# The opening and the last pair of a conditional-residual kernel: a bias row spread by TensorE, a new order of first transfers and products, and one copy moved ahead of a store

## What is computed

```python
x = x + einsum('bct,bcd->bdt', x, weights[subjects]) + bias[subjects][:, :, None]
x = x + einsum('btd,od->bto', x, W) \
      + einsum('btr,bor->bto', einsum('btd,brd->btr', x, A[adapter]), Bm[adapter]) * scalings[adapter]
```

## Time and profile before

| what | before |
|---|---|
| median of three executions | 241.67 us |
| the profiled execution's own time | 241.36 us |
| its span, first to last instruction | 239.6 us |
| TensorE (PE) matmul, busy | 229.4 us, 96% |
| VectorE (DVE) / ScalarE (ACT) / GpSimd (POOL), busy | 149.2 / 107.9 / 79.6 us |
| granted TensorE clock, mean | 0.996 |
| DMA, bytes and mean rate | 36.64 MB, 153 GB/s |

### The profile page before, as it was taken

How to read it: one execution, slowest core, us unless ns; L and a number is a source line. 1 busy time by engine, 2 the same in 40 slices (tenths; PEclk the granted TensorE clock), 3 DMA queues, 4 the chain that set the end, 5 groups by cost and what they waited for, 6 DMA issues and landing times.

```text
span 239.6 us, 9653 instructions
## 1 busy us (share of the span) xinstructions
PE 229.4 (96%) x2900; PEld 187.7 (78%) x2901; DVE 149.2 (62%) x259; ACT 107.9 (45%) x185; POOL 79.6 (33%) x277
## 2 busy tenths in 40 slices
PE   1899999999999999999999999999999999999992
PEld 1787878888887888888888888888788888888761
DVE  6799848873358636875258835875448754425762
ACT  3184663543436363562436354454435434344441
POOL 4467771700077610610056730525135131000000
PEclk9999999999999999999999999999999999999998
DMA  5956455736565474645555574645646364562233
GB/s 132 279 169 193 141 176 156 198 94 176 148 197 141 120 213 131 201 108 192 134 154 163 147 215 109 192 115 160 172 135 191 109 200 110 155 178 63 83 78 90
DMA packets 23723, 36.64 MB, mean 153 GB/s; under 512 B 6162, under 2 KB 6162, under 8 KB 23698
## 3 DMA queue, kind: packets, MB, share of 16 engines
q1 hardware_dynamic: 16480, 26.10, 40.0%
q10 hardware_dynamic: 7218, 10.23, 13.7%
HBM read 19.53 MB, written 16.78 MB: 152 GB/s over the span
## 4 chain that ended last, share of the span: by engine, by line
PE 89%; DVE 2%; DMA 2%; ACTq 2%; issue 1%; ACT 1%; DVEq 0%
PE ps L883 69%; PE ps L843 14%; PE ps L819 3%; DMA o_ring<-in_L_cond_W_dram 2%; PE ps L764 1%; ACTq L693 1%; PE ps L775 1%; DVE o_ring L554 1%; ACT x_hi L658 1%; ACT m_f L681 1%; DVE x_lo L534 0%; PE ps L813 0%; DVE last_parts L539 0%; PE ps L871 0%; DVE o_ring L549 0%
## 5 line engine op out<-in xcount | busy, mean ns | idle before, releaser
L883 PE MATMUL ps<-m_hi,x_hi 128*128 x244 | 97.0, 398 | 0.0
L883 PE MATMUL ps<-m_hi,x_lo 128*128 x244 | 95.1, 390 | 0.0
L883 PE MATMUL ps<-m_lo,x_hi 128*128 x244 | 95.1, 390 | 0.0
L534 DVE TENSOR_TENSOR x_lo<-x,x_hi 128x512 fp32r<-128x512 f32 x64 | 44.7, 698 | 62.8 <-ACT x_hi L658 62.4
L374 POOL COPY p_pair<-p_all 64x64 f32 x128 | 42.8, 335 | 113.8 <-DVE x L526 96.9
L658 ACT ACTIVATE x_hi<-x 128x512 fp32r<-128x512 f32 x64 | 40.4, 632 | 56.0 <-ACT o_ring L671 30.9
L671 ACT ACTIVATE o_ring<-ps 128x512 f32<-128x512 f32 x60 | 35.9, 598 | 52.1 <-PE ps L883 50.7
L883 PEld LDWEIGHTS ps<-m_hi,x_hi 128*128 128x128 f32 x244 | 45.8, 188 | 10.7 <-issue 0.4
L883 PEld LDWEIGHTS ps<-m_hi,x_lo 128*128 128x128 f32 x244 | 45.8, 188 | 9.7
L883 PEld LDWEIGHTS ps<-m_lo,x_hi 128*128 128x128 f32 x244 | 45.8, 188 | 9.0
L526 DVE TENSOR_TENSOR x<-ps,bias_pair 128x512 f32<-128x512 f32 x64 | 43.6, 685 | 11.1 <-PE ps L843 10.1
(11 more groups left out here) (102 smaller groups left out, 82.4 us busy)
## 6 DMA issues: line engine op xcount, KB each, us to landing
x_ring<-in_x_dram SPq DMA_DIRECT2D x122, 128.0 KB, 2.7
out_dram<-o_ring ACTq DMA_DIRECT2D x64, 128.0 KB, 2.6
out_dram<-o_ring SPq DMA_DIRECT2D x64, 128.0 KB, 2.3
a_f<-in_L_cond_A_dram SPq DMA_DIRECT2D x8, 128.0 KB, 2.7
x_ring<-in_x_dram ACTq DMA_DIRECT2D x6, 128.0 KB, 3.4
o_ring<-in_L_cond_W_dram SPq DMA_DIRECT2D x2, 256.0 KB, 4.7
o_ring<-in_L_cond_W_dram ACTq DMA_DIRECT2D x2, 256.0 KB, 5.8
b_nat<-in_L_cond_Bm_dram ACTq DMA_DIRECT2D x1, 256.0 KB, 3.7
```

The lines of the kernel that those rows point to most:

```text
L534: nc.vector.tensor_tensor(x1_lo[:, u % HELD], x1[:, u % 2], x1_hi[:, u % HELD], ALU.subtract).then_inc(x1_lo_ready, 1)
L883: mm = nc.tensor.matmul(ps[:, 2 + u % 2, :], part, m_tile(m, k, c), start=(c == 0 and part is hi and m is m_hi), stop=(c == TC - 1 and par ...
```

## The change

- SP's queue takes the weights before W tile 0, then (after a wait for GpSimd's `bias_zeroed`) a 2 KB row of all biases into row 0 of a new tile `bias_row` whose other rows are zero, then W tile 1. The transfer that read the bias 128 times is gone.
- TensorE spreads the row: `ones` (128 x 128) times `bias_row` in four products of 128 columns, two of them behind `scalings` and in front of the batch table, two behind the tables; ScalarE copies the bank to `bias_all` and signals `bias_ready`.
- `turn_w(0)` moves behind the tables, `turn_b(0)` in front of `turn_w(2)`. Three products of the identity (512 columns each) are added behind the counts.
- ScalarE reads one word for its first transfer instead of eight, and starts the lower halves of pairs 0 and 1 only; SP reads one word, then eight, and starts both halves of pairs 2 and 3. `a_round(1, 1)` moves behind ScalarE's transfer of pair 7.
- `wt` bank 3 instead of bank 0 is copied by VectorE, behind `a_split(0, 0)`.
- The rows of `a_parts` are zeroed by ScalarE (first half, in the opening) and by GpSimd (second half, after pair 3).
- In the last pair the copy of the first half's lower rows (`copy_last_low`) stands in front of `store_odd` of pair 62, and `copy_low` of the last pair copies the second half alone.

```diff
@@ -90,6 +90,7 @@
         scal_row = sb("scal_row", [1, K])
+        bias_row = sb("bias_row", [P, S * C])
         neg = sb("neg", [P, 2])
@@ -147,6 +148,9 @@
         bias_in = sem("bias_in")
+        bias_zeroed = sem("bias_zeroed")
+        bias_spread = sem("bias_spread")
+        bias_ready = sem("bias_ready")
         bnat_in = sem("bnat_in")
@@ -266,8 +270,10 @@
                 sp.dma_start(ids_i[:, 0:1], adapter.rearrange("(b a) -> b a", a=1)).then_inc(ids_in, 16)
+            sp.dma_start(p_all[0:C], w.rearrange("s c d -> c s d")).then_inc(w0_in, 16)
             sp.dma_start(w_nat[:, 0, :], W[0:P, :]).then_inc(w_in[0], 16)
-            sp.dma_start(p_all[0:C], w.rearrange("s c d -> c s d")).then_inc(w0_in, 16)
+            sp.wait_ge(bias_zeroed, 1)
+            sp.dma_start(bias_row[0:1, :], bias.rearrange("s d -> (s d)").rearrange("(a n) -> a n", a=1)).then_inc(bias_in, 16)
             sp.dma_start(w_nat[:, 1, :], W[P:2 * P, :]).then_inc(w_in[1], 16)
@@ -292,9 +298,10 @@
             load_half(sp, 0, 0, b, x_first[0])
-            b = words(sp, regs[:5], batch[0:1, 2:7], B - 1)
-            for i in range(1, XR):
-                load_half(sp, i, 0, b[2 * i - 2], x_first[i])
+            b = words(sp, regs, batch[0:1, 0:2 * XR], B - 1)
+            load_half(sp, 1, 0, b[2], x_first[1])
+            for i in range(2, XR):
+                load_x(sp, i, b[2 * i:2 * i + 2], x_first[i])
             load_a(1, 1)
@@ -331,9 +338,7 @@
             pool.wait_ge(consts, 6)
-            for half in range(2):
-                nc.gpsimd.memset(a_parts[GR - GR * half:P - GR * half, half, :].bitcast(F32), 0.0).then_inc(rows_zeroed, 1)
-                pool.wait_ge(rows_zeroed, half + 1)
+            nc.gpsimd.memset(bias_row[:], 0.0).then_inc(bias_zeroed, 1)
@@ -380,10 +385,14 @@
                 if isinstance(j, int) and j == 0:
-                    pool.wait_ge(bias_in, 16)
+                    pool.wait_ge(bias_ready, 1)
                 for half in range(2):
 ...
                                           .rearrange("p s d -> p (s d)")).then_inc(pair_ready, 1)
+                if n is None and j == HEAD - 1:
+                    pool.wait_ge(pair_ready, j * 4 + 4)
+                    nc.gpsimd.memset(a_parts[0:GR, 1, :].bitcast(F32), 0.0).then_inc(rows_zeroed, 1)
+                    pool.wait_ge(rows_zeroed, 2)
                 if n is not None and u == 7:
@@ -556,7 +565,7 @@
             dve.wait_ge(zeroed, 3)
-            dve.wait_ge(rows_zeroed, 2)
+            dve.wait_ge(rows_zeroed, 1)
             dve.wait_ge(w0_in, 16)
@@ -565,9 +574,9 @@
             b_split(0)
-            dve.wait_ge(wt_turned, 1)
-            nc.vector.tensor_copy(wt[:, 0, :], ps[:, FIRST, :]).then_inc(wt_copied_too, 1)
             a_split(0, 0)
+            dve.wait_ge(wt_turned, TC)
+            nc.vector.tensor_copy(wt[:, TC - 1, :], ps[:, FIRST + TC - 1, :]).then_inc(wt_copied_too, 1)
             x1_add(0, 0)
@@ -577,6 +586,7 @@
             x1_add(2, 2)
+            dve.wait_ge(rows_zeroed, 2)
             a_split(1, 1)
@@ -614,8 +624,6 @@
                 act.dma_start(w_nat[:, o, :], W[o * P:o * P + P, :]).then_inc(w_in[o], 16)
-            act.dma_start(bias_all[:], bias.rearrange("s d -> (s d)").rearrange("(a n) -> a n", a=1)
-                          .to_broadcast([P, S * C]).rearrange("p (s d) -> p s d", s=S)).then_inc(bias_in, 16)
             regs = [act.alloc_register(f"act_word{i}") for i in range(4)]
@@ -670,19 +678,30 @@
+            def copy_low_half(j, u, half):
+
+                i = n_of_mixed(j)
+                act.wait_ge(low_done[half][i], 1)
+                nc.scalar.activation(low[0:C, half], ps[C:2 * C, 2 + 2 * half + u % 2, :],
+                                     ACT.Copy).then_inc(low_ready, 1)
+
             def copy_low(j, u):
 ...
                 with act.If_ne(last_places[i][0], last_places[i][1]):
-                    for half in range(2):
-                        act.wait_ge(low_done[half][i], 1)
-                        nc.scalar.activation(low[0:C, half], ps[C:2 * C, 2 + 2 * half + u % 2, :],
-                                             ACT.Copy).then_inc(low_ready, 1)
+                    for half in range(2) if j < PAIRS - 1 else (1,):
+                        copy_low_half(j, u, half)
                 with act.Else():
 ...
                     nc.scalar.activation(low[0:C, 1], ps[C:2 * C, 2 + u % 2, :], ACT.Copy).then_inc(low_ready, 2)
+
+            def copy_last_low(j, u):
+
+                act.wait_ge(out_ready, j)
+                with act.If_ne(last_places[MIXED - 1][0], last_places[MIXED - 1][1]):
+                    copy_low_half(j, u, 0)
@@ -702,14 +721,19 @@
             nc.scalar.activation(scal_all[:], ps[:, 6, 0:K], ACT.Copy).then_inc(scal_ready, 1)
+            nc.scalar.activation(a_parts[GR:P, 0, :].rearrange("p (c k) -> p c k", c=TC), ones[GR:P, :].unsqueeze(1)
+                                 .to_broadcast([GR, TC, P]), ACT.Copy, scale=0.0).then_inc(rows_zeroed, 1)
             act.wait_ge(batches_ready, 1)
-            b = words(act, last_regs, batch[0:1, 0:2 * XR], B - 1)
-            for i in range(XR):
-                load_half(act, i, 1, b[2 * i + 1], x_first[i])
+            b, = words(act, regs[:1], batch[0:1, 1:2], B - 1)
+            load_half(act, 0, 1, b, x_first[0])
+            act.wait_ge(bias_spread, 1)
+            nc.scalar.activation(bias_all[:].rearrange("p s d -> p (s d)"), ps[:, 0, :], ACT.Copy).then_inc(bias_ready, 1)
+            b, = words(act, regs[1:2], batch[0:1, 3:4], B - 1)
+            load_half(act, 1, 1, b, x_first[1])
             a_round(0, 0)
+            copy_wt(0)
             copy_wt(1)
             copy_wt(2)
-            copy_wt(3)
             last_batches = words(act, last_regs, batch[0:1, B - 2 * MIXED:B], B - 1)
@@ -718,10 +742,10 @@
             b = words(act, regs[:2], batch[0:1, 4 * XR - 2:4 * XR], B - 1)
-            a_round(1, 1)
             x1_round(1, 1)
 ...
             load_x(act, XR - 1, b, x_in)
+            a_round(1, 1)
             x1_round(2, 2)
@@ -748,6 +772,8 @@
                     copy_low(j, u)
+                    if j == PAIRS - 2:
+                        copy_last_low(j + 1, u + 1)
                     store_odd(j, u, last_batches[2 * n_of_mixed(j) + 1])
@@ -777,13 +803,25 @@
+            def spread_bias(part):
+
+                cols = slice(part * P, part * P + P)
+                return nc.tensor.matmul(ps[:, 0, cols], ones[:], bias_row[:, cols], start=True, stop=True)
+
+            def keep_busy(bank, times):
+
+                for _ in range(times):
+                    nc.tensor.matmul(ps[:, bank, :], ident_b[:], ident_b[:].unsqueeze(1).to_broadcast([P, TC, P]),
+                                     start=True, stop=True)
+
+            keep_busy(FIRST, 3)
             pe.wait_ge(firsts_ready, 1)
 ...
             nc.tensor.matmul(ps[:, 6, 0:K], ones[0:1, :], scal_row[:], start=True, stop=True).then_inc(scal_spread, 1)
-            pe.wait_ge(w_in[0], 16)
-            for c in range(TC):
-                turn_w(0, c)
+            pe.wait_ge(bias_in, 16)
+            for part in range(2):
+                spread_bias(part)
             pe.wait_ge(place_ready, 1)
@@ -792,10 +830,16 @@
             mm.then_inc(others_tabled, 1)
+            for part in range(2, TC):
+                mm = spread_bias(part)
+            mm.then_inc(bias_spread, 1)
+            pe.wait_ge(w_in[0], 16)
+            for c in range(TC):
+                turn_w(0, c)
+            turn_b(0)
             pe.wait_ge(w_in[2], 16)
 ...
                 turn_w(2, c)
-            turn_b(0)
             for c in range(TC):
@@ -806,10 +850,10 @@
-                if chunk == 0:
+                if chunk == TC - 1:
                     pe.wait_ge(wt_copied_too, 1)
                 else:
-                    pe.wait_ge(wt_copied, chunk)
+                    pe.wait_ge(wt_copied, chunk + 1)
                 nc.tensor.matmul(ps[:, FIRST + chunk, :], a_parts[:, 0, chunk * P:chunk * P + P], b_parts[:],
 ...
```

## The result

The changed kernel takes 242.74 us (median of six executions, 242.54 to 243.32), the kernel before 241.53 (six, 241.25 to 241.75): ratio 1.0045, 95% interval 1.0033 to 1.0057. It is slower by 1.2 us. The profiled execution took 242.54 us with a span of 240.8, against 241.36 and 239.6.

The account below looks back on a forecast made before the run. TensorE was taken to bound the kernel, the change touching only its two ends. The end -0.7, the bias row +0.35 and SP's added transfers +0.6 gave +0.25, so 241.9 us; range 240.9 to 243.0.

Parts of the forecast that it names:

- late-row rival: Rival: bias row lands late, at 6.9, and the transfer for pairs 4 to 7 lands slower; +1.1, 242.8 us; chance 0.28.
- The last pair: Kernel's end: first half's copy ahead of the previous pair's store starts the last addition earlier; -0.7, bounds -0.6 and -0.72.
- Products behind the counts: Opening: the three 512-column identity products fall in a stretch where TensorE mostly waits; cost 0, gain 0.
- Cost nothing, gain nothing: Verdict on the three identity products in the opening: 0 in the sum; uncovered they would cost 3 x 0.24.
- Behind it TensorE has no slack to give back: From the pairs 4 to 7 stage at 21.90 on: each microsecond that stage moves is a microsecond of the whole.
- The clock in the opening: Behind the counts: clock already at 2.4 GHz, so the identity products gain nothing; the skill's half-clock rule allowed up to 0.85.
- The row in front of the table: Opening: the batch table now waits for the bias row and starts later; +0.35, bounds -0.2 and +0.7.
- B: Time at which the bias row lands in the opening: 6.45 us taken, bounds 5.9 and 6.8.
- d: Shift of the batch table's start in the opening, bias row's landing minus 6.1: +0.35 taken, bounds -0.2 and +0.7.
- TensorE's order behind the tables: Opening: with spreads and transposes moved there, pair 0's layer 0 starts at 12.2 + d; no loss besides d.
- Halves on SP: Half transfers moved from ScalarE to SP delay the last transfer for pairs 4 to 7; +0.6, bounds +0.4 and +1.3.

Follow-up runs that it names:

- e3_fill: The kernel before plus eleven 8-column TensorE products nobody reads, behind the counts: 242.39 us, ratio 1.0040 to the kernel before.
- e4_busy: The kernel before plus only the change's three 512-column identity products behind the counts: 241.69 us, ratio 0.9997 to the kernel before.
- e10_lean_nobusy: The changed kernel with one 512-column bias product behind the tables instead of four, without the identity products: 241.16 us, ratio 0.9985 to the kernel before.
- e6_fewer: The changed kernel with two 256-column bias products instead of four of 128, without the identity products: 242.19 us, ratio 1.0008 to the kernel before.
- e7_halves: The changed kernel with the lower halves of pairs 1 to 3 back on ScalarE's queue: 243.03 us, ratio 1.0057 to the kernel before.
- e9_lean: The changed kernel with one 512-column bias product behind the tables instead of four, identity products kept: 241.47 us, ratio 0.9996 to the kernel before.

## Why the prediction was right and where it was wrong

The range held the time, but the likeliest case did not come: +0.25 and "no change" were forecast, +1.2 and slower was measured. The late-row rival gave 242.8 by another road, and is not confirmed by that. That the wide range reached to 243.0 is luck as far as the 1.4 of the gap goes: no term of the sum had it. The terms that the sum did have came to -0.2 in the profile, against +0.25.

- **The last pair:** right. -0.7 forecast; -0.66 and -0.71 by itself; the lag behind TensorE's end 0.14 forecast, 0.15 found.
- **Products behind the counts and instructions added at all:** this is the step that failed. "Cost nothing, gain nothing" looked for cover for their time alone. They and the bias products are eleven products more ahead of a place in the program at which TensorE runs dry, and that cost 1.4 in the changed kernel's profile and 0.66 by the medians of `e3_fill`; the prediction had 0. "Behind it TensorE has no slack to give back" held; that nothing there would move did not.
- **The clock in the opening:** misread. I took the earlier trace rows, 1.00, and four transposes in 0.85 for full speed. The changed kernel's own rows (PE's timeline) show both levels:

```profile
3.36 1.44 PE L814 MATMUL ps<-ident_b 128*128 128x512 bf16 x3
...
11.08 0.22 PE L848 MATMUL ps<-ident_b 128*128 128x128 bf16 x1
11.13 0.39 PE L790 MATMUL ps<-ident,o_ring 128*128 128x128 f32 x2
11.36 0.22 PE L848 MATMUL ps<-ident_b 128*128 128x128 bf16 x1
```

The three products of 512 columns start 0.38 and 0.43 apart, where one of 512 columns takes 0.23 in the loop: that is the lower level, 1.2 GHz, while the granted clock reads 1.00 here as in the earlier trace rows. Later a bank (two transposes and an identity product) takes 0.28. In the kernel before, a bank takes 0.53 up to 11.6: it ran its transposes to the last at 1.2 GHz.

```profile
10.01 0.31 PE L804 MATMUL ps<-ident_b 128*128 128x128 bf16 x1
10.12 0.64 PE L764 MATMUL ps<-ident,o_ring 128*128 128x128 f32 x2
10.55 0.31 PE L804 MATMUL ps<-ident_b 128*128 128x128 bf16 x1
```

So the rule of the Trainium skill, "TensorE: Matmul & The Clock Gate", Part 1, which I set aside for the row, describes this opening: half clock until the engine has been busy. What the prediction worked out from it for the three products did not come, though (`e4_busy`, `e10_lean_nobusy`). That it is the work around the tables, the bias products first, that brings the clock up is argued from the fourteen profiles above.
- **The row in front of the table:** mechanism right, sizes off in both terms. B was 6.11, not 6.45; but two bias products and the way to the table took 1.19, not 0.66: a bias product is two products by the profile's count, 0.21 each, and the very first took 0.38. Together d = +0.6 instead of +0.35. With B = 7.2 in `e6_fewer` the upper bound of 6.8 was too low.
- **TensorE's order behind the tables:** layer 0 was forecast at 12.2 + d, which is 12.8 with the d that was measured, and started at 12.07. Two errors partly cancel: the two bias products behind the tables took 1.15, from the end of the tables on, instead of 0.43, and what follows `turn_w(0)` took 2.5 (9.58 to 12.07) instead of 3.9, since it ran at full clock from 10.42 on.
- **Halves on SP:** the place is right, the size was not +0.6. The last transfer, issued at 18.45, landed at 21.9 and the stage moved by 0.47 with d in it, because SP's one long issue, which stood among its six at 15.5, is not among them in the changed kernel (six issues in 3.88 instead of 4.71). The forecast kept it. `e7_halves` doesn't show what the halves cost by themselves, and no other run does.

## What to carry to other kernels

Where TensorE is the bound from end to end, look first behind its last product: a copy that waits behind a store it has nothing to do with was worth 0.7 here, twice, and it was priced from four rows. Before calling an instruction on the critical engine free because its time is hidden, remember that in this kernel eleven such products cost 0.66: their number decided what work met the place in the program at which the engine stood still. An idle time put down to "issue" in the middle of a steady sequence is the sign, and fewer, wider products ahead of it made it go (`e6_fewer`, `e10_lean_nobusy`) or shrink to 0.25 (`e9_lean`). Check the clock by the distance of two like products, not by the recorded grant alone, and look at the next transfer-bound stage before you spend effort on an opening.
